# A 512-wide graph layer: TensorE waits for its own counts behind three quarters of a gather round, a product and a source step

## What is computed

```python
def _gin_conv(h, src, dst, w, b, eps, n_nodes):
    agg = jax.ops.segment_sum(h[src], dst, num_segments=n_nodes)
    return ((1.0 + eps) * h + agg) @ w + b
n = x.shape[0]
h = jax.nn.relu(_gin_conv(x, src, dst, w1, b1, eps1, n))
h = jax.nn.relu(_gin_conv(h, src, dst, w2, b2, eps2, n))
return _gin_conv(h, src, dst, w3, b3, eps3, n)
```

## Time and profile before

| what | value |
| --- | --- |
| median of 3 runs | 4995.4 us (4991.88 to 4999.53) |
| span of the profiled execution, first to last instruction | 4893.1 us |
| time of the profiled execution itself | not given apart; the timed runs are 102 us over its span |
| mean granted TensorE clock | 0.886 |
| TensorE (PE) busy | 3799.9 us, 78% |
| VectorE (DVE) busy | 2235.7 us, 46% |
| ScalarE (ACT) busy | 1434.7 us, 29% |
| GpSimd (POOL) busy | 2679.8 us, 55% |
| moved by DMA | 734.87 MB, mean 150 GB/s |
| gathers of the wide layer, L2258 | 782, from 3098.6 to 4280.1 us |
| their matmuls, L2451 | 1564 pieces, 777.0 us |

### The profile page before, as it was taken

One profiled execution on the slowest core, in us unless ns is written; L12 is line 12 of the kernel. 1 busy time (PEld: TensorE's weight loads), 2 busy tenths in 40 slices (PEclk: granted clock), 3 DMA queues, 4 the chain that ended last, 5 costly groups with the idle time before them and its releaser, 6 DMA issues. The chain is left out here.

```text
span 4893.1 us, 71187 instructions
## 1 busy us (share of the span) xinstructions
PE 3799.9 (78%) x15901; PEld 2488.7 (51%) x15902; DVE 2235.7 (46%) x7891; ACT 1434.7 (29%) x2745; POOL 2679.8 (55%) x4185
## 2 busy tenths in 40 slices
PE   3886645656566556986999999688888888779999
PEld 1233324444444444875677777344444444457777
DVE  6997756767676677345121121222222222222222
ACT  3983222222222222245344444100000000023333
POOL 6781056676766666013544444266666666646664
PEclk9999977777777777985999999799998999889999
DMA  4442233333333333026767666477777776646665
GB/s 138 176 184 92 58 82 92 95 97 96 96 96 96 94 96 86 0 67 179 201 183 206 189 183 185 138 211 210 214 210 206 209 214 206 197 135 208 204 202 178
DMA packets 346846, 734.87 MB, mean 150 GB/s; under 512 B 77407, under 2 KB 171229, under 8 KB 341985
## 3 DMA queue, kind: packets, MB, share of 16 engines
q0 software_dynamic: 176144, 461.72, 33.4%
q10 hardware_dynamic: 100178, 157.63, 10.3%
q1 hardware_dynamic: 70268, 113.00, 6.7%
HBM read 622.28 MB, written 109.84 MB: 150 GB/s over the span
## 5 line engine op out<-in xcount | busy, mean ns | idle before, releaser
L900 POOL DMA_INDIRECT a_gathered<-table,record x850 | 808.2, 951 | 642.6 <-issue 378.5
L2258 POOL DMA_INDIRECT l_gathered<-table,record x782 | 761.0, 973 | 472.1 <-issue 283.4
L2451 PE MATMUL bank<-l_gathered,l_onehot 128*125 128x512 f32 x1564 | 777.0, 652 | 179.1 <-DMA l_gathered<-table,record 110.7
L1828 POOL DMA_INDIRECT l_gathered<-table,record x578 | 546.1, 945 | 463.4 <-PE bank L2036 215.9
L1249 PE MATMUL bank<-a_gathered,a_onehot 128*125 128x264 f32 x1700 | 570.3, 494 | 101.6 <-DVE a_gathered L1053 79.0
L2451 PEld LDWEIGHTS bank<-l_gathered,l_onehot 128*125 128x125 f32 x1564 | 316.3, 207 | 617.3 <-issue 457.6
L1942 ACT ACTIVATE l_part<-l_packed 128x1000 fp32r<-128x1000 bf16 (+1 forms) x396 | 413.3, 1070 | 554.4 <-PE bank L2017 227.1
L1249 PEld LDWEIGHTS bank<-a_gathered,a_onehot 128*125 128x125 f32 x1700 | 393.5, 243 | 203.9 <-issue 76.5
L2017 PE MATMUL bank<-rows_first,l_part 125*125 125x512 f32 x1650 | 406.6, 405 | 29.3 <-ACT l_part L1942 29.2
L2017 PE MATMUL bank<-rows_last,l_part 125*125 125x512 f32 x1650 | 394.5, 398 | 11.3 <-ACT l_part L1942 9.9
L2017 PEld LDWEIGHTS bank<-rows_first,l_part 125*125 125x125 f32 x1650 | 308.4, 187 | 121.2 <-issue 43.9
(11 more groups left out here) (282 smaller groups left out, 5515.3 us busy)
## 6 DMA issues: line engine op xcount, KB each, us to landing
l_packed<-adjacency ACTq DMA_DIRECT2D x265, 250.0 KB
adjacency<-d_stage SPq DMA_DIRECT2D x35, 1562.5 KB
l_packed<-adjacency ACTq DMA_DIRECT2D x132, 281.2 KB
l_gathered<-table,record POOLq DMA_INDIRECT x1360
a_gathered<-table,record POOLq DMA_INDIRECT x850
table<-rows_first POOLq DMA_DIRECT2D x50, 250.0 KB, 3.5
table<-l_work ACTq DMA_DIRECT2D x50, 250.0 KB
l_source_rows<-table ACTq DMA_DIRECT2D x50, 250.0 KB
```

What stands on the lines that cost most here:

```text
L900: pool.indirect_dma_start(out=gathered0[s][:, j * TW:(j + 1) * TW], out_offset=None, in_=table0, in_offset=bass.IndirectOffsetOnAxis(ap=re ...
L1828: pool.indirect_dma_start(out=gathered[g][:, j, :], out_offset=None, in_=table, in_offset=bass.IndirectOffsetOnAxis(ap=record[k.t][:, j, 0 ...
L2258: pool.indirect_dma_start(out=gathered[:, j * w:(j + 1) * w], out_offset=None, in_=table, in_offset=bass.IndirectOffsetOnAxis(ap=record[t] ...
L2451: last = pe.matmul(total[0:NB, 0:w], onehot[t][:, j, :], rows[:, j, :], start=False, stop=(j == T - 1), skip_group_check=True)
```

## The change

TensorE gets three kinds of waits for counts that it raises itself. After each of the first three quarters of a round it waits until its own count of used quarters shows that quarter. After the product it waits for its own count `product` (blocks 0 to 39). Before it clears the sum of a block it waits for its own count of the source step issued just before (blocks 1 to 42). Nothing else is changed; lines from L2442 on move down by two and more.

```diff
@@ -2440,6 +2440,8 @@
                         else:
                             t = record_of(s, i)
                             pe.wait_ge(sums_read[s], i + 1)
+                            if not isinstance(i, int) or 0 < 2 * i + s <= BLOCKS - AHEAD:
+                                pe.wait_ge(source_used[1 - s], i + s + AHEAD // 2 + 1)
 
                             pe.matmul(total[0:NB, 0:w], zeros[:, 0:NB], zeros[:, 0:w], start=True, stop=True)
                             with pe.Fori(lo, hi, RE) as at:
@@ -2453,6 +2455,8 @@
                                         if j == T - 2:
                                             last.then_inc(round_gathered[t], 1)
                                     last.then_inc(quarters_used, 1)
+                                    if q < NQ - 1:
+                                        wait_apart(pe, quarters_used, before * NQ + NQ + q + 1, NQ)
                                 pe.reg_add(rounds[t], rounds[t], 1)
                                 pe.reg_add(emptied, emptied, 1)
 
@@ -2488,6 +2492,8 @@
                         for k in range(4):
                             last = pe.matmul(product_ps[0:NB, 0:D], zT[s][:, k, :], w3_sb[:, k, :], start=(k == 0), stop=(k == 3))
                         last.then_inc(product[s], 1)
+                        if not isinstance(i, int) or 2 * i + s + 2 + AHEAD < BLOCKS:
+                            pe.wait_ge(product[s], i + 1)
 
                     over_steps(pe, [(rounds_of, 0), (turn, 1), (down, 2)], source_sums, 6)
```

## The result

The changed kernel took 5353.2 us (median of 4 runs, 5343.9 to 5367.9) against 4997.5 for the kernel before in the same comparison (4 runs, 4991.9 to 5006.5). The ratio is 1.0719, interval [1.0697, 1.0741]: slower by 356 us. I had forecast slower, by 164 us, with a range up to 5280; the time lies above it.

A forecast was written before the change was run, and what follows sets the result against it. POOL's gather stream plus its stand for TensorE's late count was taken as the bound, 25.0 us a block; 41 blocks growing by 4.0 us added 164 us to 4995, giving 5159 us, range 4865 to 5280.

The forecast's parts named there:

- What bounds the kernel: Wide layer: a block takes 25.0 us, 21.5 of gather stream plus POOL's stand of about 3.6 before the next.
- What holds the counts: Wide layer: POOL's running stream, not TensorE's queued work, holds TensorE's counts back; given chance 0.52.
- TensorE's running ahead: Rival, wide layer: queued pieces delay the counts, so waits free them and the kernel takes 4885 us; chance 0.36.
- The prompt wait: TensorE's wait for its own prompt count: 0.4 us each, five per block, 2.0 us.
- The product's count is late by 0.7 to 3.7, say 2.2: Wait behind the product in each wide-layer block: 2.2 us of lateness, taking TensorE from 15.6 to 17.8 after release.
- 28.9: Forecast us from one release to the end of the next first quarter, after stream end, late source count and zeros.
- 4.0: Forecast us added to each block's period, by zeros and first quarter coming after the source count; 41 blocks, 164 us.
- The source wait as the one that does it: Wait before the zeros: holds back the next first quarter, which POOL needs, and so causes the growth of 164 us.
- my upper bound for the clock (238): TensorE at its lower clock after a stand: 1.8 us more per block, 238 us in all, 5233 us.
- The upper bound: Counts of quarters two and three late by 3.7 us each: another 2.1 us per block, 5319 us; range ended at 5280.
- The 102 us around the span: Difference between the median run of 4995.4 us and the span of 4893.1, taken as time around the span.
- The check named for it: Signs in the wide layer: gathers per 200 us from 136 to about 118, POOL's stand about 7.5 us, lower clock.

The follow-up runs named there:

- p1: Kernel before, with a memset and a wait for it behind each of the 17 gathers: 4951.9 us, ratio 1.0128 to the kernel before.
- the last series: Comparison on chip 14: kernel before 4884.8 us, whole change 5242.0 us (ratio 1.0724), change without the product wait 5157.4 us (ratio 1.0554).

## Why the prediction was wrong, and where it was right

- **What bounds the kernel: right.** Single buffer, stream of 17 gathers, POOL's stand at the end of it. On a chip without held counts the stand is gone and the period is 21.5 us, as the stream alone gives.
- **What holds the counts: right in kind.** It is POOL's unbroken stream; p1 shows it by pauses, and an idle TensorE in the earlier trace rows had said so. That TensorE's running ahead is the cause fell: TensorE stood in its own wait for 10.6 us and the count didn't come. The Trainium skill's rule (Perfetto Trace Analysis, Tensor Engine Instruction: the update goes out when PSUM has acknowledged the write) matches the chips with prompt counts, 0.04 us, and not the others, with 10 us. The cycle per increment that the prediction sets beside it stands in the Trainium skill (Advanced Engine Details and Errata, DMA Bandwidth Details) among figures of DMA, not of TensorE, and no run here shows it.
- **The prompt wait: nearly right.** From start to start it is 0.27 to 0.41 us for the quarters and 0.4 to 0.6 for the product, where I took 0.4 each. The idle time that the rows show for it, 0.24 to 0.26 us, is only a part of that.
- **The step that failed: "The product's count is late by 0.7 to 3.7, say 2.2".** It is late by 10.4 us, since it too stands until the stream's end. I took the lateness from two blocks, in which the product ended 8 to 9 us into the stream, and the rest of the same trace had a median of 5.4 us. And I kept it for a schedule in which the product ends 13.8 us into the stream. With that the source step (3.75 us at the lower clock, and 0.14 before it) isn't beside the stream but between release and first quarter. My 28.9 + 3.9 = 32.8, and with 0.2 for zeros and quarter, 0.5 for a later release and 0.5 less for the stream it is the 33.0 measured. The growth is 8.0 in this block, and 8.3 on the mean of blocks 3 to 40, instead of 4.0.
- **The source wait as the one that does it: half right.** Without the product wait it costs 273 us (with the quarters), by the mechanism described, which is more than my upper bound for the clock (238). In the whole change its count is prompt, and the product wait has taken over.
- **The upper bound: too narrow.** I let the quarters' counts be late by 3.7 us, which they are not, and never the product's by more than I had seen.
- **The 102 us around the span: wrong.** Every execution on record whose span is known took 1.6 to 1.8 us more than it, so the 102 were the difference between two levels of the same kernel. It did no harm to the forecast, made as a difference, but it should have made me ask what differed.
- **The check named for it** (118 gathers in 200 us, POOL's stand 7.5 us, a lower clock) had the sign right: 104, 12.5 us, 0.82.

## What to carry to other kernels

A wait for one's own count is cheap (0.3 to 0.6 us here) only where the count is prompt. Where counts can stand until another engine's stream has ended, such a wait ties the engine to the end of that stream, and what it costs is the work queued between the wait and the thing that restarts the stream; count every piece of it, and take the lateness from where the instruction will stand in the new schedule, not from where it stood, and from many blocks, not from two. A time of a kernel whose profile and timed runs differ by 2% isn't one level: look on a second chip before an effect is called one of the program.

## What the runs showed that I had not expected

The kernel before took 4694.6 to 4697.8 us on three chips, 4883 to 4885 on two, and 4997 in the first comparison. The lower level has no late product count in the wide layer in any of its 12 traces; the upper ones, but for p1, have one in 41 to 44 of the 50 blocks. The change costs 0.1% on the one kind and 7.2% on the other, the same 7.2% at 4885 and at 4997. What parts these two upper levels lies mostly outside the wide layer: the changed kernel's gathers start 46 us later in the first comparison than in the last series, take 13 us longer, and 30 us more follow them. Why is open.

VectorE's own counts aren't held where they can be read: in the row of L2336 above it waits 0.15 us for its own count, in the middle of a stream on a chip with held counts, and as long on a chip with prompt ones.

Something else goes with the two kinds. The traces with prompt counts hold 68,152 to 68,208 records of semaphore updates, the seven with held counts 33,897 to 35,696, and p1 43,254, though the program raises the same counts wherever it runs. So on the chips with held counts about half of these records are missing, and not in the wide layer alone. The many waits there that end in "remote" fit this. All times on record, but for those of the kernel before in the first comparison, come with a span and a granted clock, so they are of executions that were recorded. Whether TensorE's counts are late on those chips, and the change costs 7.2%, when nothing is recorded, no run shows. It is a rival for why the counts stand that stays untested.

SyncE's issues are less even on the chips with held counts. Its 50 issues of one and the same DMA (shortest, median and longest in ns) in the kernel before on a chip with prompt counts:

```profile
L2213 SPq DMA_DIRECT2D l_own<-table x50: 303/306/382, 3050.6 to 4085.7; - x50
```

and in the changed kernel of the last series, with held counts:

```profile
L2213 SPq DMA_DIRECT2D l_own<-table x50: 7/324/1373, 3102.0 to 4641.2; - x50
```

The medians hardly differ; in the changed kernel of the first comparison the median is 690 ns. Whether this has the same cause as the late counts, and what makes one chip differ from another, stays open. The program can't choose the chip, and no run separated the chip from what else ran beside it. Not tried: pauses at the quarters' ends only, and a second gather buffer for the first quarter, which would let POOL go on without the late count.
